# A gated two-layer transformer on one core: attention 0 reordered, attention 1's queries prepared three units ahead on ScalarE

## The chip, the core and the metric

The kernel is one program on one core of a Trainium2 chip. The core has five engines that run their own instruction streams and meet through semaphores: TensorE (PE, matrix products and transposes; PEld is its weight load), VectorE (DVE), ScalarE (ACT), GpSimd (POOL) and SyncE (SP, here a queue that issues DMAs). The metric is the device time of one execution in microseconds, lower is better. The median of three executions of the kernel before is 2252.59 us (2250.19 to 2254.02).

## The reference, cut to what matters

Four batches of 512 tokens with 512 channels pass four layers. Each is `x = x + tanh(g) * f(layernorm(x))`:

```
attention 0:  kv  = ctx @ W_k.T + b_k                     # 512 x 128 per batch
              sim = (xn @ kv) @ kv.T * scale              # 512 x 512
              f   = softmax(normalise_rows(sim) * gamma + beta)
mixture 0:    8 experts, 2 chosen per token, and a shared network of 1024
attention 1:  16 heads of 32 in 4 groups; keys and values are the 4 x 32 columns of ctx
              f   = (softmax(q @ k.T / sqrt(32)) @ v) @ Wc.T + bc
mixture 1:    16 experts, 6 chosen per token, and a shared network of 704, with biases
```

`layernorm` subtracts the mean of a token's 512 channels and divides by their deviation; it has no parameters. All is float32; where TensorE is to be fast and exact, a number is split into a high and a low part (`hi`, `lo`) and the products of the parts are summed.

## The kernel before, in words

The four layers run one after another in blocks of their own; all engines meet between blocks. `x` stays in SBUF as `x_res`, 16 tiles of 128 tokens, four for a batch. Nothing is scheduled by a planner: each engine's instructions stand in the order in which the code writes them, and an engine that waits holds back everything behind it.

**Statistics.** `row_stats` (VectorE, L104 to L118) takes a batch's sums, ScalarE's `deviation` (L125) takes the root of the variance in between, and the last two operations leave `rstd` and `nbias`; the next step on VectorE waits for ScalarE's answer.

**Attention 0** (L210 to L478). For each batch: the keys `kvT` (TensorE L415, ScalarE L348), their mean and centred copy `kc` (L351, L357), `kvT` turned into `kv` (L418, L353); the normalised rows `xn` (L130) turned into `pT` (L425, L363); the product `oT` (L429, L367), the scores (L436) into PSUM banks 0 to 3; ScalarE squares them (L373) and takes the root (L376), VectorE scales and adds (L449 to L465), ScalarE takes the exponent (L381), VectorE adds the result to `x_res` (L470 to L476). TensorE does the keys, the turning, the product and the scores of one batch after the other in a loop. ScalarE's loop body is: normalise b+1, squares b, keys b+1, turn b+1, exponents b, product b+1. Beside it GpSimd splits seven chunks of the experts' weights (`stage`, L168 to L182), and SP stores them.

**Mixture 0** begins with `row_stats` and `deviation` of batch 0 (`NORMED` = 0) and then normalises the batch's rows; batches 1 to 3 follow between the first products. The shared network comes first (L1558, L1576), then 39 blocks of 128 gathered rows. Mixture 1 has the same form with 111 blocks; its statistics of batches 0 to 2 are taken at the end of attention 1 (`NORMED` = 3).

**Attention 1** (L481 to L1050) runs 16 units, one per batch and group of four heads. A unit is eight steps j; a step scores 1024 keys by queries (TensorE L843), takes the exponent twice, as float32 and as float16 (ScalarE L792, L796), subtracts the two on GpSimd (L738) and multiplies both parts by the values (TensorE L857). Ahead of it the maxima of the scores must be known: `raw_tensor` (TensorE L828) makes raw scores that VectorE reduces (L972), half of them in the unit before (steps 0 to 3) and the first half two units before (steps 4 to 7). So the raw scores of unit u+2 begin in step 4 of unit u. They need that unit's queries as strips: GpSimd centres and scales 128 channels of `x_res` (`prepare_pool`, L686, L694, at step 5 of unit u-1), TensorE turns them (`prepare_tensor`, L817, step 0 of unit u), ScalarE and VectorE take the high and low part (L756 at step 1, L961 at step 2), and SP copies them by three DMAs of 256 KB from `qhi` and `qlo` into `qs` (`strips`, L622, L625). The maxima follow as two small DMAs (`maxima`, L632). In units 0 to 3 and 12 to 15 ScalarE and VectorE also split 16 chunks of weights (`a_stage`). The values are loaded by ScalarE's queue at the start of the block (L771) and split into three parts (L777, L723, L781, L726); the first unit's products need them.

## Time and profile before

| | |
|---|---|
| median of three executions | 2252.59 us |
| profiled execution, its own time | 2243.46 us |
| its span, first to last instruction | 2241.7 us |
| PE, PEld busy | 1911.8 (85%), 1567.9 us |
| DVE, ACT, POOL busy | 1167.9, 861.3, 1004.7 us |
| mean granted TensorE clock | 0.925 |

Busy time is what an engine executes; waiting and issuing don't count. The granted clock is a share of TensorE's full speed: 1.00 is 2.4 GHz and 0.50 is 1.2 GHz, the two levels it has; a value between is a mean over time at both. Attention 0 runs from 0 to 123 us, mixture 0 to 688, attention 1 to 1170, mixture 1 to the end.

### The profile page before, as it was taken

Reading aid. Unit: us, or ns where it says so; the run is one execution under the profiler, and the core shown is the slowest. Engines: PE = TensorE matmul, PEld = TensorE weight load, DVE = VectorE, ACT = ScalarE, POOL = GpSimd, SP = SyncE. Lnnn points to the kernel's source line nnn. Section 1 sums busy time; section 2 is a strip of 40 time slices with the busy share of each in tenths; the row PEclk is TensorE's granted clock in tenths of the full one; section 3 lists DMA queues with packets and bytes.
Section 4 is the critical chain, followed back from the end, with each engine's and each line's share of the span. In section 5 each row is a group of like instructions: output and inputs, shape, how many; then the busy total and the mean of one; then the engine's idle time right before and its main releaser. Section 6 shows DMA issues by size and latency. Waiting matters only on the chain. (4 is left out here: it accounts for less than half of the span.)

```text
span 2241.7 us, 36800 instructions
## 1 busy us (share of the span) xinstructions
PE 1911.8 (85%) x10825; PEld 1567.9 (70%) x10825; DVE 1167.9 (52%) x2331; ACT 861.3 (38%) x1403; POOL 1004.7 (45%) x735
## 2 busy tenths in 40 slices
PE   3758999979892777888868899999999979999995
PEld 2347787757671455555546777799999879899994
DVE  5474654423334896878973766444444334344442
ACT  3752221123341676767655123133333223233331
POOL 4344655625454787889631001143433323333331
PEclk9779999988895798998989999999999989999998
DMA  9367666988887574323642000766469895754444
GB/s 337 122 218 242 184 205 226 294 295 240 257 197 169 151 227 98 47 42 51 190 150 83 29 31 1 264 178 158 88 176 334 265 304 128 187 130 83 78 79 111
DMA packets 131457, 372.67 MB, mean 166 GB/s; under 512 B 20456, under 2 KB 24424, under 8 KB 126104
## 3 DMA queue, kind: packets, MB, share of 16 engines
q1 hardware_dynamic: 80504, 260.69, 36.3%
q0 software_dynamic: 33600, 79.73, 18.6%
q10 hardware_dynamic: 17184, 30.09, 3.8%
q8 instruction: 96, 1.57, 0.3%
q14 instruction: 73, 0.60, 0.1%
...
## 5 line engine op out<-in xcount | busy, mean ns | idle before, releaser
L1650 PE MATMUL ps<-f_wb,f_xThi 128*128 x2088 | 537.7, 339 | 29.9 <-issue 26.8
L1774 POOL DMA_INDIRECT y_scratch<-f_yo,f_rows x150 | 238.7, 1591 | 479.0 <-issue 264.1
L1650 PEld LDWEIGHTS ps<-f_wb,f_xThi 128*128 128x128 f32 x2088 | 372.0, 193 | 41.3 <-issue 32.3
L1650 PE MATMUL ps<-f_wb,f_xTlo 128*128 x1044 | 346.7, 332 | 0.0
L738 POOL TENSOR_TENSOR a_elo<-a_e,a_ehi 128x1024 f16<-128x1024 f32 x128 | 282.8, 2222 | 87.0 <-ACT a_ehi L796 85.0
L1669 PE MATMUL ps<-f_wb,f_hThi 128*128 (+2 forms) x822 | 276.9, 418 | 7.3 <-DVE f_hTlo L2049 7.3
L2067 DVE TENSOR_TENSOR f_g<-ps,f_bb 128x352 f32<-128x352 f32 x111 | 58.3, 525 | 337.2 <-PE ps L1650 334.4
L1747 POOL DMA_INDIRECT f_xg<-xn_scratch,f_rows x150 | 160.0, 1067 | 158.7 <-PE ps L1634 119.3
L1650 PEld LDWEIGHTS ps<-f_wb,f_xTlo 128*128 128x128 f32 x1044 | 200.9, 192 | 0.0
L1485 ACT ACTIVATE f_yo<-ps,f_share 128x512 f32<-128x512 f32 x150 | 103.2, 688 | 249.2 <-PE ps L1669 191.3
L972 DVE TENSOR_REDUCE a_nmax<-ps 128x1 f32<-128x512 f32 x256 | 163.9, 680 | 56.4 <-PE ps L828 56.0
L1558 PE MATMUL ps<-f_xhi,f_w13hi 128*128 128x512 f32 x448 | 175.7, 392 | 0.0
L1558 PE MATMUL ps<-f_xlo,f_w13hi 128*128 128x512 f32 x448 | 174.8, 390 | 0.0
L1558 PE MATMUL ps<-f_xhi,f_w13lo 128*128 128x512 f32 x448 | 174.7, 390 | 0.0
L1669 PEld LDWEIGHTS ps<-f_wb,f_hThi 128*128 128x128 f32 (+2 forms) x822 | 142.4, 191 | 42.3 <-issue 24.0
L1576 PE MATMUL ps<-f_w2hi,f_act_parts 128*128 128x512 f32 x448 | 153.0, 409 | 21.2 <-DVE x_res L2015 20.5
L828 PE MATMUL ps<-a_ks,a_qs 96*128 96x512 f32 x256 | 114.4, 515 | 61.1 <-DMA a_qs<-a_qlo 41.9
L792 ACT ACTIVATE a_e<-ps 128x1024 f32<-128x1024 f32 x128 | 132.7, 1036 | 82.5 <-PE ps L843 81.0
L1473 ACT CAST f_xThi<-ps 128x512 fp32r<-128x512 f32 x150 | 88.1, 587 | 195.1 <-PE ps L1634 187.7
L1669 PE MATMUL ps<-f_wb,f_hTlo 128*128 (+2 forms) x411 | 162.2, 395 | 0.0
L1479 ACT CAST f_hThi<-ps 128x384 fp32r<-128x384 f32 (+1 forms) x150 | 67.4, 449 | 207.5 <-PE ps L1659 202.7
L2049 DVE TENSOR_TENSOR f_hTlo<-ps,f_hThi 128x384 fp32r<-128x384 f32 (+1 forms) x150 | 78.4, 523 | 113.7 <-ACT f_hThi L1479 111.6
...
## 6 DMA issues: line engine op xcount, KB each, us to landing
...
```

Of the source, the lines that this page charges most:

```text
L738: pool.tensor_tensor(l, e, h, ALU.subtract).then_inc(lo_pool, 1)
L792: act.activation(e32[:, j % 4, :, :], ps[:, 2 * (j % 2):2 * (j % 2) + 2, :], ACT.Exp)
L828: pe.matmul(ps[:, A_BANK + n % 2, :], qs[0:3 * HD, HPG * grp + q, P * t:P * t + P], ks[0:3 * HD, grp, :], start=True, stop=True).then_inc( ...
L972: dve.tensor_reduce(nmax[:, grp % 2, n:n + 1], ps[:, A_BANK + n % 2, :], AX.X, ALU.max, negate=True).then_inc(max_done, 1)
L1473: act.copy(xThi[:, b % 2, :, :].rearrange("p k t -> p (k t)"), ps[:, XB, :]).then_inc(xT_hi, 1)
L1485: act.activation(yo[:, b % 3, :], ps[:, OB + b % 2, :], ACT.Identity, scale=share[:, b:b + 1]).then_inc(yo_ready, 1)
L1558: mm = pe.matmul(ps[:, 2 * h + w, :], wt[:, h, w, k, :], xt[:, k, S * t:S * t + S], start=(m == 0), stop=(m == 3 * KD - 1))
L1576: mm = pe.matmul(ps[:, bank(c), :], at[:, t % 2, h, P * c:P * c + P], wt[:, h, :], start=(m == 0), stop=(m == 5))
L1650: mm = pe.matmul(out, xt[:, b % 2, k, :], weights(at, w, k, low), start=(m == 0), stop=(m == 3 * KD - 1))
L1669: mm = pe.matmul(ps[:, OB + b % 2, :], ht[0:n, b % 2, P * j:P * j + P], wb[0:n, bass.ds(at + 512 * NB + 1024 * j + 512 * low, D)], start=( ...
L1747: pool.indirect_dma_start(xg[:, b % 3, :], None, xn_d, bass.IndirectOffsetOnAxis(ap=rows_of[:, b:b + 1], axis=0), bounds_check=ROWS + SPAR ...
L1774: pool.indirect_dma_start(y_d, bass.IndirectOffsetOnAxis(ap=rows_of[:, b:b + 1], axis=0), yo[:, b % 3, :], None, bounds_check=ROWS + SPARE ...
```

## The change

**Attention 0.** `kv` and `kc` get a buffer per batch, the keys use banks 4 to 7 in turn, and all four batches' keys are made ahead of the first product. The loop is written out, with no keys in it; TensorE turns batch b+1 right behind the scores of b, and the product starts as soon as the first of the four columns is copied. Batch 0 turns ahead of the third `deviation`. The statistics that mixture 0 wants of batches 0 to 2 are taken in attention 0's loop, one batch late, and `NORMED` is 3 for both mixtures.

**Attention 1.** `prepare_pool` is gone. ScalarE makes the same columns with one operation per 128 tokens (`columns_scalar`) at step 4 of the unit, four units ahead; transposes, parts and strips are made for unit u+3 at the steps where they were made for u+2. At the start three units' strips are made; the values are loaded by SP behind the strips of units 0 and 1, and ScalarE splits them behind its other first work.

```diff
-        kc = sb(ctx, "a0_kc", [P, S])
+        kc = sb(ctx, "a0_kc", [P, B, S])
...
+                act.activation(kvT[:], ps[:, 4 + 2 * (b % 2), :], ACT.Identity, bias=bk[:, 0:1],
                                accum_out=ksum[:]).then_inc(kvT_ready, 1)
                 act.wait_ge(kvT_ready, b + 1)
                 act.mul(nmean[:], ksum[:], -1.0 / S).then_inc(nmean_ready, 1)
+                act.wait_ge(nmean_ready, b + 1)
...
                 act.wait_ge(kv_tr, b + 1)
-                act.copy(kv[:].rearrange("p t d -> p (t d)"), ps[:, 5, :]).then_inc(kv_ready, 1)
-
-                act.wait_ge(nmean_ready, b + 1)
-                act.wait_ge(sim_ready, TB * b + TB)
-                act.activation(kc[:], kvT[:], ACT.Identity, bias=nmean[:, 0:1]).then_inc(kc_ready, 1)
+                act.copy(kv[:, b, :, :].rearrange("p t d -> p (t d)"), ps[:, 5 + 2 * (b % 2), :]
+                         ).then_inc(kv_ready, 1)
...
+                    act.copy(pT[:, k, :], ps[:, turned_bank(b) + k, :]).then_inc(pT_ready, 1)
...
+                    act.wait_ge(sim_ready, TB * b + t + 1)
...
+                if b > 0:
+                    g["deviation"](act, 1, b - 1)
...
                 g["deviation"](act, 0, 0)
+                normalise_scalar(act, 0)
                 act.wait_ge(par_in, PARAMS)
-                normalise_scalar(act, 0)
                 keys_scalar(act, 0)
                 g["deviation"](act, 0, 1)
+                keys_scalar(act, 1)
+                turn_scalar(act, 0)
                 g["deviation"](act, 0, 2)
-                turn_scalar(act, 0)
+                keys_scalar(act, 2)
                 g["deviation"](act, 0, 3)
+                keys_scalar(act, 3)
                 act.wait_ge(scale_in, SCALES)
                 act.activation(gates[:], graw[:], ACT.Tanh).then_inc(gates_ready, 1)
                 product_scalar(act, 0)
...
+                    if b == 0:
+                        pe.wait_ge(kv_ready, B)
+                    for k in range(KD):
+                        pe.wait_ge(pT_ready, KD * b + k + 1)
+                        mm = pe.matmul(ps[:, 4, :], kv[:, b, k, :], pT[:, k, :], start=(k == 0), stop=(k == KD - 1))
+                    mm.then_inc(oT_mm, 1)
...
+                pe.wait_ge(par_in, PARAMS)
+                keys(0)
+                keys(1)
+                turn(0)
+                keys(2)
+                keys(3)
+                for b in range(B):
+                    product(b)
+                    scores(b)
+                    if b + 1 < B:
+                        turn(b + 1)
...
-                dve.sem_inc(sim_used, TB)
...
-                with dve.Fori(0, B) as b:
+                for b in range(B):
+                    if b > 0:
+                        g["row_stats"](dve, 1, b - 1)
...
                 load(1, 1)
                 strips(0, 0)
                 strips(1, 1)
+                for b in range(B):
+                    sp.dma_start(vraw[:, TB * b:TB * b + TB, :],
+                                 a["ctx_512"][b, :, :].rearrange("(t p) d -> p t d", p=P)).then_inc(v_in, 16)
                 load(2, 2)
+                strips(2, 2)
                 sp.dma_start(wcT[:], a["a1_wcT"].rearrange("(k p) n -> p k n", p=P)).then_inc(par_in, 16)
                 sp.dma_start(bc[:], a["a1_bc"].to_broadcast([P, D])).then_inc(par_in, 16)
                 maxima(0, 0)
...
-                    if has_prepare:
-                        strips(u + 2, (grp + 2) % GROUPS)
-                        if not (static and u + 3 == UNITS):
-                            load(u + 3, (grp + 3) % GROUPS)
+                    if not (static and u + 3 >= UNITS):
+                        strips(u + 3, (grp + 3) % GROUPS)
+                        load(u + 3, (grp + 3) % GROUPS)
...
-                pool.wait_ge(g["s_ln"], 2 * B + 1)
-                for u in range(2):
-                    prepare_pool(pool, u, u, 0)
...
-                prepare_pool(pool, 2, 2, 0)
...
-                        if j == 5 and has_columns:
-                            b3 = (0 if wc_batch is None else wc_batch + 1) + (grp + 3) // GROUPS
-                            prepare_pool(pool, u + 3, (grp + 3) % GROUPS, b3)
...
+            def columns_scalar(act, u, grp, b):
+
+                wait(act, q_tr, u - 1)
+                for t in range(TB):
+                    T = TB * b + t
+                    act.activation(xc[:, grp % 2, t:t + 1, :].rearrange("p o (d q) -> p o d q", q=HPG),
+                                   x[:, bass.ds(T, 1), P * grp:P * grp + P].rearrange("p o (q d) -> p o d q", q=HPG),
+                                   ACT.Identity, scale=rstd[:, bass.ds(T, 1)],
+                                   bias=nbias[:, bass.ds(T, 1)]).then_inc(xc_ready, 1)
...
+                act.wait_ge(g["s_ln"], 2 * B + 1)
+                for u in range(2):
+                    columns_scalar(act, u, u, 0)
                 keys_scalar(act, 0, 0)
                 keys_scalar(act, 1, 1)
                 prepare_scalar(act, 0, 0)
+                columns_scalar(act, 2, 2, 0)
+                prepare_scalar(act, 1, 1)
+                columns_scalar(act, 3, 3, 0)
+                prepare_scalar(act, 2, 2)
+                g["deviation"](act, 2, 2)
                 act.wait_ge(v_in, 16 * B)
                 act.copy(v_hi, v_raw).then_inc(vhi_ready, 1)
-                prepare_scalar(act, 1, 1)
-                g["deviation"](act, 2, 2)
                 act.wait_ge(vres_ready, 1)
                 act.copy(v_mid, v_res).then_inc(vmid_ready, 1)
                 maxima_scalar(act, 0, 0)
                 g["deviation"](act, 2, 3)
+                act.wait_ge(g["s_ln"], 2 * B + B)
...
-                        if j == 1 and has_prepare:
-                            prepare_scalar(act, u + 2, (grp + 2) % GROUPS)
+                        if j == 1 and not (isinstance(u, int) and u + 3 >= UNITS):
+                            prepare_scalar(act, u + 3, (grp + 3) % GROUPS)
+                        if j == 4 and not (isinstance(u, int) and u + 4 >= UNITS):
+                            columns_scalar(act, u + 4, grp, b + 1)
...
+                pe.wait_ge(qlo_ready, 2)
+                prepare_tensor(pe, 2, 2)
                 raw_tensor(pe, 0, 0, range(16))
-                pe.wait_ge(qlo_ready, 2)
+                pe.wait_ge(qlo_ready, 3)
...
+                    turns = not (isinstance(u, int) and u + 3 >= UNITS)
...
-                        if j == 0 and has_prepare:
+                        if j == 0 and turns:
                             if last_job(grp, b):
                                 job_read(pe, *last_job(grp, b))
                             else:
                                 pe.wait_ge(mlo_ready, u + 1)
-                            prepare_tensor(pe, u + 2, (grp + 2) % GROUPS)
+                            prepare_tensor(pe, u + 3, (grp + 3) % GROUPS)
...
                             if job(grp, 2, b):
                                 job_read(pe, *job(grp, 2, b))
                             else:
-                                pe.wait_ge(qlo_ready, u + 3)
+                                pe.wait_ge(qlo_ready, u + 4)
...
+                prepare_vector(dve, 2, 2)
...
-                        if j == 2 and has_prepare:
-                            prepare_vector(dve, u + 2, (grp + 2) % GROUPS)
+                        if j == 2 and not (isinstance(u, int) and u + 3 >= UNITS):
+                            prepare_vector(dve, u + 3, (grp + 3) % GROUPS)
...
-    NORMED = B - 1 if layer == 1 else 0
+    NORMED = B - 1
```

TensorE in attention 0, before: the loop's body up to the product (ps is PSUM, a_xn the normalised rows, a_pT these turned; ISA and REGISTER_ALU rows are the loop's waits).

```order
L415 MATMUL ps<-a_ctxT,a_wkT 128x512
L416 REGISTER_ALU
L418 MATMUL ps<-ident,a_kvT 128x128 x4
L423 ISA
L425 MATMUL ps<-ident,a_xn 128x128 x4
L423 REGISTER_ALU
L425 MATMUL ps<-ident,a_xn 128x128 x4
L423 REGISTER_ALU
L425 MATMUL ps<-ident,a_xn 128x128 x4
L423 REGISTER_ALU
L425 MATMUL ps<-ident,a_xn 128x128 x4
L429 MATMUL ps<-a_pT,a_kv 128x512 x4
```

And after, from the last batch's keys on:

```order
L426 MATMUL ps<-a_ctxT,a_wkT 128x512
L431 MATMUL ps<-ident,a_kvT 128x128 x4
L450 MATMUL ps<-a_pT,a_kv 128x512 x4
L461 MATMUL ps<-a_kc,a_oT 128x512 x4
L440 MATMUL ps<-ident,a_xn 128x128 x16
L450 MATMUL ps<-a_pT,a_kv 128x512 x4
L461 MATMUL ps<-a_kc,a_oT 128x512 x4
L440 MATMUL ps<-ident,a_xn 128x128 x16
```

The keys' two rows have left the loop; scores of a batch (L461) and the turning of the next (L440) now stand side by side.

ScalarE at the start of attention 1, before (a_v is the values' parts, a_vraw their load, a_ks the keys, a_qhi the queries' high part):

```order
L771 DMA a_vraw<-in_ctx_dram 128x4x128 x4
L750 CAST a_ks<-a_kraw 96x512 x2
L756 ACTIVATE a_qhi<-ps 128x512
L777 CAST a_v<-a_vraw 128x64x32
L756 ACTIVATE a_qhi<-ps 128x512
L125 ACTIVATE std<-vraw,eps 128x4
L781 CAST a_v<-a_vres 128x64x32
L762 CAST a_mhi<-ps 16x128
L125 ACTIVATE std<-vraw,eps 128x4
L792 ACT_TABLE_LOAD
```

And after:

```order
L768 ACTIVATE a_xc<-x_res,nbias,rstd 128x128 x8
L761 CAST a_ks<-a_kraw 96x512 x2
L777 ACTIVATE a_qhi<-ps 128x512
L768 ACTIVATE a_xc<-x_res,nbias,rstd 128x128 x4
L777 ACTIVATE a_qhi<-ps 128x512
L768 ACTIVATE a_xc<-x_res,nbias,rstd 128x128 x4
L777 ACTIVATE a_qhi<-ps 128x512
L125 ACTIVATE std<-vraw,eps 128x4
L803 CAST a_v<-a_vraw 128x64x32
L805 CAST a_v<-a_vres 128x64x32
L783 CAST a_mhi<-ps 16x128
L125 ACTIVATE std<-vraw,eps 128x4
```

Sixteen column operations are new (L768), the load is gone from this queue, and both value copies (L803, L805) moved behind three units' queries. The copy of the maxima (a_mhi) stands behind them as before.

ScalarE in unit 0 around steps 3 to 6, before (a_e and a_ehi are the two exponents):

```order
L796 ACTIVATE a_ehi<-ps 128x1024
L172 CAST a_stage_down<-a_later_raw 128x512
L792 ACTIVATE a_e<-ps 128x1024
L796 ACTIVATE a_ehi<-ps 128x1024
L792 ACTIVATE a_e<-ps 128x1024
L796 ACTIVATE a_ehi<-ps 128x1024
L168 CAST a_stage_up<-a_later_raw 128x4x4x32
L762 CAST a_mhi<-ps 16x128
L792 ACTIVATE a_e<-ps 128x1024
L796 ACTIVATE a_ehi<-ps 128x1024
```

And after:

```order
L821 ACTIVATE a_ehi<-ps 128x1024
L172 CAST a_stage_down<-a_later_raw 128x512
L817 ACTIVATE a_e<-ps 128x1024
L821 ACTIVATE a_ehi<-ps 128x1024
L768 ACTIVATE a_xc<-x_res,nbias,rstd 128x128 x4
L817 ACTIVATE a_e<-ps 128x1024
L821 ACTIVATE a_ehi<-ps 128x1024
L168 CAST a_stage_up<-a_later_raw 128x4x4x32
L783 CAST a_mhi<-ps 16x128
```

Four column operations stand between the exponents of step 4 and step 5, in each unit up to 11; the rest is unchanged.

## Rows read from the trace of the kernel before

In the windows a row gives start:end and length, then the busy us of PE, PEld, DVE, ACT and POOL with their instruction counts, the granted clock, the DMA share and GB/s. In the lines a row is line, engine, operation, tiles, shapes and count, then busy us and mean ns of one, then the engine's idle time ahead of them and what ended it. In the timeline it is start, duration, engine, line, operation.

**Rows 1.** windows, two stages: busy PE, PEld, DVE, ACT, POOL; clock; DMA

```profile
122.00:688.00 566.00, 494.33 (x2280) 397.30 (x2280) 245.30 (x522) 168.64 (x320) 289.01 (x258) 0.93 0.78 237
735.00:1142.00 407.00, 329.81 (x2735) 224.63 (x2735) 338.04 (x524) 289.70 (x363) 330.23 (x168) 0.88 0.48 119
```

**Rows 2.** windows, attention 1 by units (0-3, 4, 7-8, 9-10, 11, 12-15)

```profile
735.00:840.50 105.50, 79.04 (x648) 55.97 (x648) 97.37 (x147) 79.06 (x105) 88.25 (x44) 0.85 0.70 194
840.50:868.90 28.40, 18.98 (x174) 13.76 (x173) 14.30 (x31) 16.66 (x21) 20.63 (x11) 0.82 0.58 156
...
920.70:967.10 46.40, 37.86 (x347) 27.66 (x346) 33.84 (x63) 33.81 (x41) 42.63 (x23) 0.89 0.32 43
967.10:1017.90 50.80, 45.51 (x363) 28.27 (x362) 42.48 (x67) 33.14 (x40) 40.73 (x22) 1.00 0.25 39
1017.90:1041.20 23.30, 19.24 (x175) 14.18 (x174) 17.75 (x33) 17.16 (x22) 21.42 (x12) 0.85 0.32 43
1041.20:1140.60 99.40, 81.12 (x653) 54.37 (x652) 88.47 (x120) 75.34 (x97) 74.67 (x36) 0.85 0.58 163
```

**Rows 3.** waits, attention 1: who waited for whom, total us, times, longest

```profile
PE ps L828 <- DMA a_qs<-a_qlo: 34.2, 9, 8.3
```

**Rows 4.** lines, attention 1: xcount | busy us, mean ns | idle before

```profile
L738 POOL TENSOR_TENSOR a_elo<-a_e,a_ehi 128x1024 f16<-128x1024 f32 x128 | 282.8, 2222 | 87.0 <-ACT a_ehi L796 85.0 <-POOL a_ks L701 1.3
L996 DVE TENSOR_TENSOR a_otok<-a_osum,a_rden 128x128 f32<-128x128 f32 x62 | 62.5, 1008 | 0.4
L686 POOL TENSOR_TENSOR a_xc<-x_res,rstd 128x512 f32 (+1 forms) x13 | 17.9, 1373 | 0.0
L694 POOL TENSOR_TENSOR a_xc<-a_xc,nbias 128x512 f32<-128x512 f32 x13 | 14.7, 1128 | 2.6 <-POOL a_xc L686 2.6
L762 ACT CAST a_mhi<-ps 16x128 fp32r<-16x128 f32 x15 | 3.7, 249 | 23.0 <-PE ps L833 23.0
```

**Rows 5.** timeline, attention 0: start us, us, engine line op, count, [idle before <-releaser]

```profile
36.00 5.74 PE L429 MATMUL ps<-a_pT,a_kv 128*128 128x512 f32 x8 [14.97 <-ACT a_pT L363]
41.77 0.60 ACT L367 ACTIVATE a_oT<-ps 128x512 f32<-128x512 f32 x1 [2.19 <-PE ps L429]
42.42 3.70 PE L436 MATMUL ps<-a_kc,a_oT 128*128 128x512 f32 x8 [0.69 <-ACT a_oT L367]
51.23 3.67 PE L425 MATMUL ps<-ident,a_xn 128*128 128x128 f32 x16 [0.75 <-ACT a_kv L353]
...
92.73 0.18 DVE L449 RECIPROCAL a_rstd<-a_sdev 128x4 f32<-128x4 f32 x1 [7.56 <-ACT a_sdev L376]
98.90 0.27 DVE L465 TENSOR_SCALAR a_nmx<-a_mx 128x1 f32<-128x1 f32 x2
105.98 0.60 ACT L367 ACTIVATE a_oT<-ps 128x512 f32<-128x512 f32 x1 [1.25 <-PE ps L429]
```

**Rows 6.** timeline, first 34 us, VectorE

```profile
21.66 11.82 DVE L110 TENSOR_TENSOR mdif<-mdif 128x4 f32<-128x4 f32 x1
```

**Rows 7.** timeline, start of mixture 0

```profile
123.39 1.28 ACT L125 ACT_TABLE_LOAD   x1 [2.83 <-PEq L272]
127.55 1.52 ACT L130 ACTIVATE f_xn<-x_res,nbias,rstd 128x512 f32<-128x512 f32 x2 [0.57 <-DVE nbias L118]
143.43 0.30 ACT L125 ACTIVATE std<-vraw,eps 128x4 f32<-128x4 f32 x1 [3.52 <-DVE vraw L112]
147.58 0.78 PE L1558 MATMUL ps<-f_xhi,f_w13hi 128*128 128x512 f32 x1
```

**Rows 8.** timeline, start of attention 1

```profile
708.29 3.94 POOL L723 TENSOR_TENSOR a_vres<-a_vraw,a_v 128x2048 f32<-128x2048 f32 x1 [0.84 <-PE ps L817]
715.90 1.22 PE L828 MATMUL ps<-a_ks,a_qs 96*128 96x512 f32 x2 [7.64 <-DMA a_qs<-a_qlo]
729.71 0.25 ACT L762 CAST a_mhi<-ps 16x128 fp32r<-16x128 f32 x1 [12.84 <-PE ps L833]
735.05 1.02 ACT L792 ACTIVATE a_e<-ps 128x1024 f32<-128x1024 f32 x1
```

94 lines of the change are left out of this document (38 added, 56 removed).

## The prediction

> **What bounds the kernel now.** I read the windows by stage first. In mixture 0 TensorE is busy for 494.3 of 566.0 us [rows 1]; the change touches nothing of it but its start, and nothing of mixture 1. Attention 1 takes 407 us with no engine full: VectorE 338.0, GpSimd 330.2, TensorE 329.8, ScalarE 289.7, at a granted clock of 0.88 [rows 1]. Split by units [rows 2] it has three kinds. Units 0 to 3: VectorE 97.4 of 105.5 us, so VectorE sets the pace. Units 9 and 10, and 5 and 6 like them: TensorE 45.5 of 50.8 us, at full clock. Units 4, 7, 8 and 11 (98.1 us): TensorE idles at a clock of 0.82 to 0.89, GpSimd is busy for 84.7. The waits name one cause: TensorE's raw scores wait 34.2 us, in 9 places, for the strips of the low part [rows 3]. In attention 0 the timeline shows a chain that runs from engine to engine: the first `oT` copy at 41.77, the fourth at 105.98, so 21.4 us per batch [rows 5].
>
> **Attention 0, the loop.** It loses the keys, whose handing to and fro stood between scores and product. I lay the new loop out from one `oT` copy to the next. ScalarE: copy 0.6, four normalisations at 0.76 [rows 7], four squares at 0.6, like the copy of as many columns [rows 5], a table load of 1.28 (as [rows 7] shows one) and one or two roots of 0.30: VectorE gets the deviation at 7.5 to 7.8. VectorE needs 6.4 us from there to the last maximum (92.73 to 99.17) [rows 5]: 14.1. Two exponents follow, 1.6 by the normalisations' length, then the copy: 15.8. TensorE's path is shorter: 0.65, scores 3.7, turning 3.67, the first column's copy 0.6, product 5.74 [rows 5]: 14.4. The moved `row_stats` of a batch fits between VectorE's last addition and the next deviation, but its root stands ahead of that deviation on ScalarE, 0.3 us. I take 16.0 per batch, three times: (21.4 - 16.0) x 3 = -16.2 us; at the end +0.3.
>
> **Attention 0, the start.** Before, VectorE stood for 11.82 us in an operation on 128 x 4 numbers [rows 6], and ScalarE behind it. Now ScalarE turns batch 0 ahead of that wait. But the first product needs all four batches' keys, and the last of them stands on ScalarE behind the fourth `deviation`. If the stall comes back on a later statistics operation (GpSimd's run of work is where it was), the fourth root comes at about 37.3 and the keys take 3 us more: product at 40.3, against 36.00 [rows 5], +4.3. Without the stall 36, +0. Nothing in the trace decides; I take +2.5. Sum of attention 0: -13.4, between -17 and -5.
>
> **Mixture 0's start.** ScalarE's first instruction is at 123.39, the rows begin at 127.55, 4.16 us later [rows 7]; with statistics ready they begin at +0.35: -3.8. Later ScalarE stands 3.52 us for the third batch's statistics, and the logits' copy behind it [rows 7], of which 3.0 were behind the logits' end; that wait goes too. The first expert product, at 147.58 or +24.2 [rows 7], comes at about +17.4: -6.8. What is late next is the expert weights' load, asked for at the block's start. If that binds only half is won: -7.5 to -2.
>
> **Attention 1, the start.** Values no longer compete with the keys' load, and ScalarE does the columns at once: I expect the first strips 2 us earlier than their landing before 715.90 [rows 8]. Against this, the DMA queue holds a third unit's strips (3 x 256 KB) and the values ahead of the maxima's small copies, and ScalarE's copy of the maxima, at 729.71 before [rows 8], stands behind both value copies, which end at about 731.5 (the values in at 723.5, behind six strips; a copy of some 2 us, GpSimd's subtraction of 3.94 [rows 8], a second copy). So the first exponent, 735.05 before [rows 8], comes at 736.9: +1.8, between -3 and +5.
>
> **Attention 1, the units.** GpSimd loses 1.37 + 1.13 = 2.50 us per unit [rows 4]. ScalarE gains four operations of 128 x 128. Below they cost 0.25 each, what a 16 x 128 copy takes [rows 4], above 0.76, the 128 x 512 form with the same scale and bias [rows 7]. I take 0.40: the lower row has the same length, and a scale and a bias read from memory come on top. So 1.6 us per unit, 1.0 to 3.0. ScalarE has room: 79.1 of 105.5 us at its fullest [rows 2].
>
> The strips get a whole unit more, so the 34.2 us of waits go. What is late next differs by kind.
> - Units 4, 7, 8, 11: GpSimd (84.7 - 10.0) / 4 = 18.7 us, ScalarE (67.6 + 6.4) / 4 = 18.5, TensorE at full clock about 16.4 (its busy time by its clock). Three engines near 18 don't fit perfectly; I take 20.5 per unit: 82.0 for 98.1, -16.
> - Units 0 to 3: VectorE idles 8.1 us in all [rows 2]. Part of it goes, and with less work on GpSimd a little of VectorE's waiting for it: its operation L996 has a mean of 1008 ns [rows 4] for 128 x 128 numbers. I take -7.
> - Units 5, 6, 9, 10: TensorE's own work leaves 5.3 us of 50.8 [rows 2]; with somewhat fewer waits for VectorE -2.6 over both pairs.
> - Units 12 to 15: 99.4 us, VectorE 88.5; unit 13 no longer prepares. -2.4.
>
> Together -28; the ends are -38 (20.5 becomes 19.3, and VectorE's waits halve) and -12 (new waits between the engines take the place of most).
>
> A rule that speaks against the move: the Trainium skill (ScalarE: Activation LUTs, Rules for kernel authors) gives additions and multiplications to VectorE, not ScalarE. In units 0 to 3 this trace has VectorE at 92% and ScalarE at 75% [rows 2]. By the rule the work would be on VectorE and lengthen those units; by the rows it belongs where it is put.
>
> **Sum.** -13.4 - 6.8 + 1.8 - 28 = -46.4. The profiled execution took 2243.46 us, 9.1 below the median of 2252.59; 2243.5 - 46.4 = 2197.1 there, and 2206 for the median.
>
> **Rivals.**
> A: the engines block each other where the strips' wait stood. VectorE with two operands in SBUF waits for GpSimd already (L996, mean 1008 ns, 62 times [rows 4]), and eight columns of L738 at 2222 ns are 17.8 us per unit. For it: in units 0 to 3 only 8.1 us of VectorE's time are free. Against: units 4, 7, 8, 11 have VectorE at 14 to 18 us. Units then give -10 in place of -28: 2252.6 - 28.4 = 2224.
> B: the long stall [rows 6] strikes inside attention 0's loop, where two of the moved `row_stats` now run beside GpSimd's splitting: 2 x 11.8 = +23.6, so 2252.6 - 22.8 = 2230. The stall ended when GpSimd's run of work ended, and stretched over many of its instructions. For it: in the old place it did happen. Against: it happened once, and the batches end beyond most of GpSimd's work. The Trainium skill (SBUF, State Buffer, Who interferes with whom) says that the blocked side waits while the other's instruction holds the pair. By it each such wait would be one instruction of GpSimd, at most 2.2 us here, and the total 2 x 5 x 2.2 = 22 at the very worst; the row's 11.82 us doesn't agree with a wait for one instruction.
> C, slower: the clock. TensorE's 329.8 us in attention 1 are at 0.88 [rows 1], 290 at full clock. If shorter, more evenly spread pauses kept it at 0.7, it would be busy 414 us and with some 40 of waits take 454: +47 in place of -28, 2252.6 - 18.4 + 47 = 2281. It turns slower than before as soon as the units lose more than 18 us, a clock below some 0.75 (290 / 385). For it: 0.82 in unit 4 after a wait of 8.3 us [rows 2, 3]. Against: what preceded the low clock there was idle time, which the change takes away.
> D: the change doesn't do what it says. The wait is only booked on the strips, and something behind them (the maxima of the same unit) binds at once: the units give 0, so 2252.6 - 18.4 = 2234.
> E: all ends good: -17 - 7.5 - 3 - 38 = -65, 2188.
>
> **How the numbers follow.** Forecast (sum between -36 and -56) 0.55, A 0.20, B 0.07, C 0.03, D 0.05, E 0.07; the last 0.03 is for a loss that I don't see. The time is the first's, 2206; its own range is 2196 to 2217. The range of 8 in 10 reaches E and over A, B and D: 2187 to 2236. What lies outside is C, the unseen, and the far ends of the others, 2 in 10 at most. A measurement here tells about 0.2% (4.5 us) from no change: faster is all but C, the unseen and a little of D: 0.92; same 0.03; slower 0.05.
>
> **What would show it.** In the profile after: `oT` copies 16 us apart, the first at 42 to 46; attention 0 ending near 110; no root in mixture 0's first 20 us, first expert product 17 us behind the block's start; in attention 1 no TensorE wait for `a_qlo` behind unit 0, units 4, 7, 8, 11 near 20.5 us, GpSimd at 19 us per unit, the column operations at 0.4 us; a clock above 0.9 from unit 4 on. The forecast is wrong if the strips' wait goes and another of its size stands under DVE `a_nmax` or ACT `a_ehi` (A), if a statistics operation takes over 5 us (B), or if the clock falls (C).

## The result, and the profile after

The changed kernel took 2214.5 us (median of 6 runs, 2210.7 to 2224.1); beside it the kernel before took 2251.4 (2237.6 to 2261.3). The ratio is 0.9843, with a 95% interval of 0.9816 to 0.9870: 37 us faster, 8.5 us behind the forecast of 2206 and inside its range. A second series gave the same two kernels 2227.0 against 2252.9, ratio 0.9875 (0.9846 to 0.9904). Over both, the 12 runs of the changed kernel have a median of 2219.7: some -33 us. The difference is clear of the noise; its size is known to some 5 us only.

The profiled execution after took 2224.05 us (span 2222.2, granted clock 0.923), the slowest of its six, and the one before was 9 us quicker than its median. A difference of these two executions (19.4 us) tells too little. So I read the instants that divide the stages off the timelines of all the profiles that were taken: oT copies, first expert product, first statistics of attention 1, its first and last exponent. The first two columns are the two executions that the prediction speaks of. The means are over every profile whose code for that stage, and for what starts it, is the old or the new.

| stage, us | before | after | old code, mean (profiles) | new code, mean (profiles) | difference | forecast |
|---|---|---|---|---|---|---|
| start to the first oT copy | 41.8 | 44.6 | 42.0 (3) | 45.3 (6) | +3.3 | +2.5 |
| first to fourth oT copy | 64.2 | 52.8 | 63.3 (3) | 52.2 (6) | -11.1 | -16.2 |
| fourth copy to first expert product | 41.6 | 40.4 | 41.2 (3) | 40.0 (6) | -1.3 | +0.3 - 6.8 |
| first expert product to attention 1's statistics | 540.8 | 545.8 | 543.0 (3) | 546.3 (6) | +3.3 | 0 |
| statistics to first exponent | 46.7 | 47.3 | 46.3 (3) | 47.4 (7) | +1.1 | +1.8 |
| attention 1's units | 405.6 | 378.7 | 406.2 (3) | 377.2 (6) | -29.1 | -28 |
| mixture 1 | 1101.0 | 1112.7 | 1101 to 1118 in all fourteen | | 0 | 0 |
| sum | | | | | -33.7 | -46.4 |

The sum of the means agrees with the timing. In the row from the first expert product on, old and new profiles overlap (540.8 to 544.3 against 542.1 to 552.8), so its +3.3 is not clear of the spread. Now the stages in the profile after. The timeline of attention 0 (start us, us, engine line op, count, [idle before <-releaser]):

```profile
24.08 9.19 DVE L117 TENSOR_SCALAR rstd<-inv 128x4 f32<-128x4 f32 x1
31.99 1.25 POOL L182 TENSOR_TENSOR a_stage_down<-a_stage_raw,a_stage_down 128x512 fp32r<-128x512 f32 x1
36.62 0.30 ACT L125 ACTIVATE std<-vraw,eps 128x4 f32<-128x4 f32 x1 [10.65 <-DVE vraw L112]
39.43 5.11 PE L450 MATMUL ps<-a_pT,a_kv 128*128 128x512 f32 x8 [0.68 <-ACT a_kv L364]
44.57 0.60 ACT L375 ACTIVATE a_oT<-ps 128x512 f32<-128x512 f32 x1 [3.68 <-PE ps L450]
61.05 0.57 ACT L375 ACTIVATE a_oT<-ps 128x512 f32<-128x512 f32 x1
63.29 3.39 DVE L513 SCALAR_TENSOR_TENSOR x_res<-a_y,a_coef,x_res 128x512 f32<-128x512 f32 x2
80.25 0.57 ACT L375 ACTIVATE a_oT<-ps 128x512 f32<-128x512 f32 x1
```

The stall is back on another statistics instruction, 9.19 us on 128 x 4 numbers, and ends at 33.27 with GpSimd's last subtraction of its run (33.24). Three periods follow, 16.5, 19.2 and 17.1 us (the fourth copy is at 97.39), where I had laid out 16.0. In the second, two additions to x that need 1.41 us beside an idle GpSimd take 3.39. But in the third GpSimd runs nothing at all and no operation of VectorE is stretched. VectorE waits 4.08 us for a root on ScalarE, and ScalarE before that for TensorE's scores. The scores of this batch (first row), and of the same batch in act_cols_2 (second row; a run of experiment 2, with the same attention 0):

```profile
80.93 6.52 PE L461 MATMUL ps<-a_kc,a_oT 128*128 128x512 f32 x8 [6.26 <-issue]
82.56 3.67 PE L461 MATMUL ps<-a_kc,a_oT 128*128 128x512 f32 x8 [2.35 <-issue]
```

They take 6.52 us at a granted clock of 0.56 in the one and 3.67 at 1.00 in the other. The four batches of the profile after have 3.67, 5.89, 6.52 and 6.49 us, and TensorE stood idle for 0.73, 5.60, 6.26 and 3.87 us just before them; in the kernel before it was 3.70 us each time, behind 0.69 us of idle time. The new order made this pause: the product of a batch now runs early, so that nothing stands right before its scores. The squares on ScalarE wait for the scores, and VectorE gets the deviation 9.7 to 10.1 us behind the oT copy and not the 7.45 of the first period. The third period of the six profiles with this attention 0 follows it: 17.3, 17.1 and 17.4 us with scores of 6.7, 6.5 and 6.7, then 16.0 and 15.9 with 5.4 and 5.3, and 14.9 with 3.67. The length of the pause alone doesn't settle the clock: before the last scores it was 3.64 us in stats_in_mixture, and they took 3.67, and 3.87 us in the profile after, where they took 6.49.

The start of mixture 0 in the timeline, against [rows 7]:

```profile
117.25 0.39 SPq L1281 DMA_DIRECT2D f_gw<-in_f_gateT_dram  x1
117.31 1.52 ACT L130 ACTIVATE f_xn<-x_res,nbias,rstd 128x512 f32<-128x512 f32 x2 [2.73 <-PEq L271]
125.25 1.05 ACT L1369 CAST f_w13hi<-f_wraw 128x1024 fp32r<-128x1024 f32 x1 [0.81 <-DMA f_wraw<-in_f_w_dram]
127.70 1.04 ACT L1369 CAST f_w13hi<-f_wraw 128x1024 fp32r<-128x1024 f32 x1 [1.40 <-DMA f_wraw<-in_f_w_dram]
130.50 0.63 PE L1557 MATMUL ps<-f_xhi,f_gwlo 128*128 128x512 f32 x1
132.57 0.81 ACT L130 ACTIVATE f_xn<-x_res,nbias,rstd 128x512 f32<-128x512 f32 x1 [1.64 <-DMA xn_scratch<-f_xn]
133.79 0.59 ACT L1378 COPY f_lgT<-ps 128x512 f32<-128x512 f32 x1 [0.40 <-ACT f_xn L130]
137.75 0.54 PE L1589 MATMUL ps<-f_xhi,f_w13hi 128*128 128x512 f32 x1
```

The rows begin at once, and no root is there. But the first product comes 20.5 us behind the block's start, not 17.4: the logits are done at 131.1 and their copy waits on ScalarE to 133.79. ScalarE has stood 0.81 and 1.40 us for the load of the experts' weights, f_wraw, for which it did not wait before, and then 1.64 us for the store of an earlier f_xn, where it waited for the statistics before. All six profiles with this code have these three waits (0.8 to 1.8, 1.4 to 1.5, 1.2 to 1.7 us).

Attention 1 by the same kinds of units as [rows 2] (units 0 to 3; 4; 5 and 6; 7 and 8; 9 and 10; 11; 12 to 15), in the windows view (length, busy us of each engine, clock, DMA share, GB/s):

```profile
730.80:832.40 101.60, 80.33 (x647) 57.77 (x648) 94.36 (x144) 86.58 (x120) 76.42 (x36) 0.79 0.74 203
832.40:855.60 23.20, 20.09 (x174) 15.09 (x174) 18.95 (x34) 18.68 (x25) 17.68 (x9) 0.85 0.78 202
855.60:903.20 47.60, 43.96 (x363) 28.25 (x362) 38.72 (x67) 36.80 (x47) 37.01 (x19) 1.00 0.26 43
903.20:945.40 42.20, 35.62 (x348) 25.97 (x347) 35.23 (x61) 37.37 (x50) 36.74 (x19) 0.96 0.36 49
945.40:993.10 47.70, 44.07 (x363) 28.29 (x362) 39.14 (x69) 36.85 (x48) 37.44 (x19) 1.00 0.27 42
993.10:1013.40 20.30, 17.67 (x174) 13.49 (x173) 17.46 (x33) 18.78 (x25) 18.66 (x10) 0.92 0.36 50
1013.40:1109.50 96.10, 78.41 (x653) 53.46 (x652) 83.42 (x120) 74.41 (x96) 72.89 (x34) 0.88 0.54 161
```

The waits in it, where [rows 3] had 34.2 us for the strips (who waits for whom: us, times, longest):

```profile
PE ps L855 <- DVE a_nmax L1002: 21.9, 20, 2.9
PE ps L884 <- DVE a_osum L1018: 16.9, 12, 2.9
```

And two groups of the lines view, beside [rows 4]:

```profile
L1026 DVE TENSOR_TENSOR a_otok<-a_osum,a_rden 128x128 f32<-128x128 f32 x62 | 60.3, 973 | 0.4
L768 ACT ACTIVATE a_xc<-x_res,nbias,rstd 128x128 f32 (+1 forms) x48 | 25.8, 637 | 0.0
```

The strips' waits are gone. What TensorE waits for now is VectorE: its maxima, sums and rows of a_otok together held it for 28.2 us before (14.7 + 10.2 + 3.3) and for 45.4 after (21.9 + 16.9 + 6.6), so that 17 of the 34 us came back in pieces of 2.9 us at most. GpSimd is at 296.8 / 16 = 18.6 us per unit, as forecast. A column operation takes 25.8 / 48 = 0.54 us of ScalarE (0.64 us from its start to its end; they overlap).

### The profile page after: what moved, and what is told of

Its sections match the earlier page's. It is cut to its first block and busy times, and to the rows that moved or that the text cites. A ratio compares the mean times of both kernels' runs of the same rounds, so it can differ in the third digit from the quotient of the medians.

```text
span 2222.2 us, 36653 instructions
## 1 busy us (share of the span) xinstructions
PE 1907.8 (86%) x10825; PEld 1568.1 (71%) x10825; DVE 1152.9 (52%) x2331; ACT 891.1 (40%) x1466; POOL 967.7 (44%) x703
## 5 line engine op out<-in xcount | busy, mean ns | idle before, releaser
L1681 PEld LDWEIGHTS ps<-f_wb,f_xThi 128*128 128x128 f32 x2088 | 373.7, 194 | 40.7 <-issue 31.7
L752 POOL TENSOR_TENSOR a_elo<-a_e,a_ehi 128x1024 f16<-128x1024 f32 x128 | 282.2, 2217 | 82.7 <-ACT a_ehi L821 80.4
L1516 ACT ACTIVATE f_yo<-ps,f_share 128x512 f32<-128x512 f32 x150 | 103.3, 689 | 253.9 <-PE ps L1700 189.8
L1607 PE MATMUL ps<-f_w2hi,f_act_parts 128*128 128x512 f32 x448 | 154.0, 411 | 23.3 <-DVE x_res L2046 22.4
L884 PEld LDWEIGHTS ps<-a_v,a_ehi 128*128 128x128 f16 x1024 | 96.1, 105 | 63.1 <-DVE a_osum L1018 33.4
L855 PE MATMUL ps<-a_ks,a_qs 96*128 96x512 f32 x256 | 109.7, 498 | 34.5 <-DVE a_nmax L1002 27.9
## 6 DMA issues: line engine op xcount, KB each, us to landing
f_wb<-w_scratch SPq DMA_DIRECT2D x8, 1536.0 KB, 10.2
```

The source lines that it names most:

```text
L752: pool.tensor_tensor(l, e, h, ALU.subtract).then_inc(lo_pool, 1)
L855: pe.matmul(ps[:, A_BANK + n % 2, :], qs[0:3 * HD, HPG * grp + q, P * t:P * t + P], ks[0:3 * HD, grp, :], start=True, stop=True).then_inc( ...
L884: mm = pe.matmul(ps[:, PV_BANK, P * t:P * t + VC], part[:, j % 4, i, P * t:P * t + P], v3[:, bass.ds(TB * b + 2 * (j % 2) + i, 1), grp, 0:VC],
L1516: act.activation(yo[:, b % 3, :], ps[:, OB + b % 2, :], ACT.Identity, scale=share[:, b:b + 1]).then_inc(yo_ready, 1)
L1607: mm = pe.matmul(ps[:, bank(c), :], at[:, t % 2, h, P * c:P * c + P], wt[:, h, :], start=(m == 0), stop=(m == 5))
L1681: mm = pe.matmul(out, xt[:, b % 2, k, :], weights(at, w, k, low), start=(m == 0), stop=(m == 3 * KD - 1))
```

## The experiments

**1. The halves by themselves.** att0_only puts the old `cross_attention_1` into the changed kernel, att1_only the new one into the kernel before.

```
-def cross_attention_1(...):   # the changed one
+def cross_attention_1(...):   # the one of before          (att0_only; att1_only the other way)
```

> The changed kernel with attention 1 as it was before the change: only attention 0 and mixture 0's statistics are new. Theory S (the stages add up): the profiles after and before differ by -9.9 us from the start to mixture 0's first expert product (first oT copy +2.8, three batches -11.4, the end +2.4, mixture 0's start -3.7), and this all reaches the end, so about 2241 against 2251, ratio 0.9956, between 0.994 and 0.997. Rival R (given back later): mixture 0's experts took 545.8 us after and 540.8 before, from first product to first statistics; if they end by the transfers of the weights and not by TensorE, half or all of the gain is lost there: ratio 0.998 to 1.000, and then attention 1 alone must give some -32 to -37 us. In the profile S wants the stretch from the first expert product to attention 1's first statistics at 541 us, as before, R at 546 or more.

> The kernel before with attention 1 of the changed kernel; attention 0 and mixture 0's statistics are as before. Theory S: attention 1's units gave -26.9 us between the two profiles and its start +0.6, so -26.3: about 2225 against 2251, ratio 0.988, between 0.986 and 0.990. Rival R: -32 to -37, ratio 0.984 to 0.986. In the profile the units take 379 us (first exponent to last statistics) and mixture 1 the 1101 us that it took before; if mixture 1 takes 1112 us again, the changed attention 1 has lengthened it.

Measured: att0_only 2247.6 (12 runs) against 2255.2, ratio 0.9978 (0.9956 to 1.0000); att1_only 2220.7, ratio 0.9855 (0.9828 to 0.9882). By the ratios attention 1 is worth some -33 us and attention 0 some -5 (by the medians -34.5 and -7.6). att1_only's ratio lies in R's range and below S's, att0_only's between the two; the intervals reach into both theories' ranges. The profile of att0_only has its first expert product at 139.3, 8.3 us earlier than before, and its first exponent at 731.0, 4 us earlier: mixture 0 took 545.9. So part of the gain is lost there, as R has it, not all. In att1_only the units took 374.3 us, 5 less than S expected. Mixture 1 took 1114 us in both, not S's 1101; the profiles of experiment 4 bear on this.

**2. The lead and the move apart.** pool_cols_3 keeps the lead of three units and gives the columns of units 4 to 15 back to GpSimd; act_cols_2 keeps the columns on ScalarE and goes back to two units.

```
 pool_cols_3, GpSimd:  + if j == 5 and u + 4 < UNITS: columns_pool(pool, u + 4, grp, b + 1)
              ScalarE: - if j == 4 ...: columns_scalar(act, u + 4, grp, b + 1)
 act_cols_2, SP:       - strips(u + 3, ...)            + strips(u + 2, ...)
             ScalarE:  - prepare_scalar(act, u + 3, .) + prepare_scalar(act, u + 2, .)   (TensorE, VectorE alike)
```

> The changed kernel, but with the columns of units 4 to 15 on GpSimd again (two wide operations behind its sixth subtraction of a unit), still three units ahead; the first four units' columns stay on ScalarE. Theory L (the lead of a unit is what gains): the strips' waits stay away, and GpSimd is busy for 2.5 us more of each of 12 units, 21 to 21.5 us per unit. Units 0 to 3 and 12 to 15, where VectorE sets the pace, and 5, 6, 9, 10, where TensorE does, change by under 2 us together; units 4, 7, 8, 11 become GpSimd's at 21.2 to 22.5 us, 87 to 90 for 85.7. So +3 to +6 us over the changed kernel, about 2219, ratio 0.986 to the kernel before. Rival M (the move off GpSimd is what gains): of the 27 us of the units 15 or more come from GpSimd's 2.5 us times 16 less, the units then take 394 us and more, 2230, ratio 0.991.

> The changed kernel, but turned and copied into strips two units ahead as before (columns made one unit less ahead too), with the columns on ScalarE. Theory L: TensorE's waits for a_qlo are back at 25 to 35 us in some 9 places, units 4, 7, 8, 11 take 94 to 98 us in all, the units 395 to 402 us: 2233 to 2238, ratio 0.992 to 0.994 to the kernel before. Rival M: the strips' wait returns only in part because GpSimd no longer delays the low parts, units at 384 to 388 us, about 2222, ratio 0.987. The values are loaded behind two units' strips, so attention 1's first exponent comes up to 2 us earlier than in the changed kernel by either.

Measured: pool_cols_3 2239.4, ratio 0.9929 (0.9897 to 0.9961); act_cols_2 2239.1, ratio 0.9937 (0.9916 to 0.9958). Of the units' -27 us between these two profiles (405.6 to 378.7) each edit alone gives a part: 398.9 and 395.1 us. By kinds of units:

| units, us | GpSimd, two (before) | GpSimd, three | ScalarE, two | ScalarE, three (after) |
|---|---|---|---|---|
| 0 to 3 | 105.4 | 111.5 | 105.1 | 101.6 |
| 4, 7, 8, 11 | 98.1 | 85.0 | 96.0 | 85.6 |
| 5, 6, 9, 10 | 102.6 | 103.3 | 96.2 | 95.4 |
| 12 to 15 | 99.5 | 99.1 | 97.8 | 96.1 |

The second row is the lead's, -13 against -2 for the move alone. For act_cols_2 theory L came out in its waits, its units and its ratio; its waits show TensorE again at

```profile
PE ps L853 <- DMA a_qs<-a_qlo: 33.9, 9, 5.6
```

The third row is the move's alone, -6 to -8, and there my theory L was wrong for pool_cols_3 (and so were its 87 to 90 for the second row: GpSimd had the room). The units' 398.9 us and the time are worse than even M's 394 and 2230. Units 5 and 6 of pool_cols_3 in the windows and lines views:

```profile
865.10:916.40 51.30, 45.57 (x364) 28.30 (x364) 42.84 (x67) 33.20 (x40) 43.27 (x24) 1.00 0.24 40
...
L1044 DVE TENSOR_TENSOR a_otok<-a_osum,a_rden 128x128 f32<-128x128 f32 x8 | 9.5, 1188 | 0.0
```

and the same two units of the profile after:

```profile
L1026 DVE TENSOR_TENSOR a_otok<-a_osum,a_rden 128x128 f32<-128x128 f32 x8 | 5.5, 686 | 0.0
```

The eight multiplications that read two tiles in SBUF lose 4 us, as much as the pair of units (51.3 to 47.6) and as VectorE's busy time (42.8 to 38.7). GpSimd no longer runs the four column operations of the pair (2.7 + 2.1 us), and the multiplications are caught beside one of its instructions less often: alone they take 0.28 us, caught up to 1.9.

The first row needs both edits: the lead alone costs 6 us, together they win 4. The lines view of these units names where, in pool_cols_3 and in the profile after (VectorE's part of the weights' splitting):

```profile
L182 DVE TENSOR_TENSOR a_stage_down<-a_later_raw,a_stage_down 128x512 fp32r<-128x512 f32 x7 | 18.3, 2615 | 0.0
L182 DVE TENSOR_TENSOR a_stage_down<-a_later_raw,a_stage_down 128x512 fp32r<-128x512 f32 x7 | 4.7, 678 | 0.0
```

In pool_cols_3 each of the seven starts some 0.1 to 0.3 us behind a GpSimd subtraction (L770) and takes 2.6 us; after, each takes 0.68. Before the change half of the eight took 1.82, beside GpSimd's column operations. That is 13.6 us more of VectorE, whose waits TensorE then has: 27.5 us there, 18.8 after. The cost is one of timing between two engines; no run moves only this operation.

**3. The stall at the start.** late_staging makes GpSimd wait for the fourth row_stats before it splits anything; att0_early leaves the stall and puts the first product, its scores and squares ahead of keys 2 and 3 (in banks 6 and 7). all_starts has both, and two edits in attention 1. after_again is the changed kernel again, the control of this series.

```
 late_staging, GpSimd:  + pool.wait_ge(g["s_ln"], B)
 att0_early, TensorE:     turn(0); - keys(2); keys(3); product(0); scores(0)
                                   + product(0) (waits kv_ready 1); scores(0); keys(2); keys(3)
             ScalarE:     turn_scalar(0); + normalise(1); product_scalar(0); squares(0); deviation(2); keys(2); ...
 all_starts, att. 1:      VectorE row_stats(2, 2) ahead of prepare_vector(2); ScalarE maxima_scalar(0) ahead of v_mid
```

> The changed kernel once more, as the control of this call and for a second profile of it. Both theories: ratio to the kernel before 0.984, between 0.982 and 0.987, some 2215. What it tells apart is what of the first profile belongs to the kernel and what to one execution: the units at 379 +- 3 us; mixture 1 again at 1110 to 1115 us, as in five profiles of five different kernels, so that the 1101 of the kernel before was the exception (theory S: mixture 1 is not touched), or at 1101 (rival: its length goes its own way from execution to execution).

> The changed kernel, with GpSimd's splitting of the bias rows and of the weights in attention 0 held back until all four row_stats are done. Theory P (the stall is GpSimd's run of wide operations: it ended at 33.19 with GpSimd's last subtraction at 33.24, and at the same place before): no operation on 128 x 4 takes over 0.7 us, batch 3's root comes at 27.6 and not at 36.6, the first product at some 30.5, the first oT copy at 35.6 and not at 44.6, -9; GpSimd catches up, since it idles for 44 us at the end of attention 0, but more of its work stands beside VectorE's in the first batch, +1 to +3: in all -6 to -8 us, ratio 0.981. Rival Q (the stall is something else of the start, a load that lands late on a shared queue, or the first use of an instruction): the stall stays at 9 us under another statistics operation and the first oT copy at 44 to 46, ratio 0.984 to 0.986.

> The changed kernel with attention 0's beginning in another order: the first product, its scores and their squares come ahead of the third and fourth batch's keys and deviations, which go to banks 6 and 7. The stall stays. Theory E (what the stall holds back is only the chain through batch 3's root): the first product starts at 24 to 25 and the first oT copy is at 29 to 31 and not at 44.6; VectorE begins batch 0's y at 37.5 to 38.5 and not at 52, and the second oT copy comes at 50 to 54 and not at 61: -8 to -10 us at the second copy and everywhere behind it, ratio 0.980. Rival F (it comes back behind the copy): keys 2 and 3 and the tanh now stand on ScalarE between deviation and exponents, and TensorE turns batch 1 only behind them: second copy at 57 or later, under -4 us, ratio 0.982 to 0.984.

> Both edits of attention 0's beginning (GpSimd's splitting held back, first product ahead of the last keys), and in attention 1 batch 2's statistics moved ahead of the third unit's low parts (VectorE idles there for 6.0 us) and the maxima's copy ahead of the second value copy on ScalarE. Theory: without the stall the statistics end near 28, y of batch 0 starts at 34 to 35, the second oT copy at 48 to 51: -10 to -12 us; attention 1's first exponent comes 42.5 to 43.5 us behind the first statistics and not 47.3, -4; in all -14 to -16 us, ratio 0.977 to 0.978, about 2200. Rival: mixture 0's experts hand half of it back (from first product to statistics 545 us and more with the earlier start, 541 to 544 with the later ones so far): -8, ratio 0.981.

Measured against 2252.9: after_again 2227.0, ratio 0.9875 (0.9846 to 0.9904); late_staging 2217.3, 0.9833 (0.9804 to 0.9862); att0_early 2212.6, 0.9820 (0.9788 to 0.9853); all_starts 2217.3, 0.9828 (0.9796 to 0.9860). The control missed its range by a hair; its units (381.0 us) and its mixture 1 (1111.9) are as expected. P is shown: the timeline of late_staging has

```profile
25.84 0.17 DVE L117 TENSOR_SCALAR rstd<-inv 128x4 f32<-128x4 f32 x1
30.88 1.26 POOL L333 TENSOR_TENSOR a_b2s<-a_b,a_b2s 16x512 fp32r<-16x512 f32 x1
35.57 0.60 ACT L376 ACTIVATE a_oT<-ps 128x512 f32<-128x512 f32 x1 [2.27 <-PE ps L451]
50.51 0.57 ACT L376 ACTIVATE a_oT<-ps 128x512 f32<-128x512 f32 x1
53.42 2.73 DVE L514 SCALAR_TENSOR_TENSOR x_res<-a_y,a_coef,x_res 128x512 f32<-128x512 f32 x2
59.61 1.25 POOL L182 TENSOR_TENSOR a_stage_down<-a_stage_raw,a_stage_down 128x512 fp32r<-128x512 f32 x1
71.44 0.57 ACT L376 ACTIVATE a_oT<-ps 128x512 f32<-128x512 f32 x1
```

No stall, and the first copy at the 35.6 that I expected (batch 3's root at 29.4 for 27.6, the product at 31.8 for 30.5). The first period is 14.9 us, with scores of 3.67 and GpSimd idle for most of VectorE's part of it (42.8 to 47.8); the second, beside GpSimd's deferred work and with scores of 6.5, 20.9, of which VectorE is busy for 20.2 (windows). Of the 9.0 and 9.4 us won at the first copy 8.3 and 9.2 are left at the first expert product (129.4 against 137.8 and 138.7). In att0_early the first copy is at 28.3 and the second at 48.6, and the product comes at 125.8; By these instants E is right, F wrong; the ratio lies between the two. all_starts has them at 26.3 and 45.8, but 68.5 and 87.9 behind that: without the stall GpSimd's work meets VectorE in the loop, where two additions to x took 5.96 us, and its product (129.0) is 3 us later than with att0_early alone. Its theory (0.977) is missed and its rival met, 0.981 with mixture 0 at 545 us and more; in attention 1 the first exponent came 46.8 us behind the statistics and not the 42.5 to 43.5 expected, on which the next experiment bears. The intervals of the three overlap that of the control; for their order the instants in the profiles speak, not the timing. Mixture 0 took 548.0 to 551.1 us in these three, and 541 to 546 in most of the others (552.8 in after_again).

**4. The mixtures, the moved statistics, and attention 1's start.** before_again is the kernel before; stats_in_mixture has row_stats of batches 0 to 2 back in mixture 0; start_queue and early_and_queue change attention 1's start.

```
 stats_in_mixture:  - NORMED = B - 1                      + NORMED = B - 1 if layer == 1 else 0
                    - row_stats(dve, 1, b - 1), deviation(act, 1, b - 1)   (attention 0)
 start_queue, SP:   - wcT, bc; maxima(0, 0)               + maxima(0, 0); wcT, bc   (waited for from unit 4 on)
              and the two edits of all_starts in attention 1; early_and_queue adds att0_early
```

> The kernel before once more, for a second profile of it. Theory S: its ratio is 1.000 within 0.3%, and mixture 1 takes 1110 to 1118 us, as in the nine profiles of other kernels, none of which changes mixture 1; the 1101 of the first profile were that one execution. Mixture 0 takes 541 to 544 us from first expert product to attention 1's statistics, with 15 to 18 us of waits for gathered rows, as in the two profiles with the old attention 0. Rival R2: mixture 1 takes 1101 again, then the old start together with the old attention 1 really leaves it shorter by 11, and mixture 0 545 or more would say that the longer waits for gathered rows don't come from attention 0's earlier end.

> The changed kernel with batch 0 to 2's row_stats back at mixture 0's start. Theory W (the wait that they left is taken by another, so the move gains little): mixture 0's first expert product comes 24 us behind the block's first instruction, as before, against 20.5 with them moved; attention 0's loop is 0 to 1 us shorter per batch without them, 51 to 52.8 for three, and its end 1 to 2 us shorter. From the fourth oT copy to the first product 41.5 to 43 us against 40.3 and 40.7. In all 0 to +2 us to the changed kernel. Rival V (the move is worth the 6.8 us that were forecast): from the fourth copy to the product 46 or more.

> The changed kernel, with three edits at attention 1's start: batch 2's statistics ahead of the third unit's low parts, the maxima's copy on ScalarE ahead of the second value copy, and the loads of wcT and bc (1.25 MB) issued behind the maxima's two small copies and waited for only from unit 4 on. Theory K (the maxima's copies stood behind these transfers: in the run before with the first two edits the low parts of the maxima were ready at 718.2 and on their way at 718.9, and TensorE waited 5.67 us for them, to 724.3): the wait falls to about 2.1 us, as where the queue is empty, and the first exponent comes 42.5 to 43.5 us behind the first statistics, not 46.8 to 47.3. -4 us to the changed kernel. Rival N (it is the values and the third unit's strips, 1.8 MB, that fill the queue): TensorE waits 4 us or more and the first exponent stays at 45 to 47.

> The first product ahead of the last keys in attention 0, and the three edits at attention 1's start: the version that the runs point to. From att0_early (2213, ratio 0.982) and theory K's -4: about 2208, ratio 0.980, 0.977 to 0.983. Rival: mixture 0's waits for gathered rows and the rest of the program give it back, ratio 0.983 and more.

Measured against 2252.5: before_again 2253.4, ratio 1.0009 (0.9989 to 1.0028); stats_in_mixture 2224.4, 0.9877 (0.9837 to 0.9916; 4 runs); start_queue 2219.5, 0.9858 (0.9829 to 0.9888); early_and_queue 2209.4, 0.9824 (0.9792 to 0.9856).

before_again took 1110.9 us in mixture 1 and 544.3 in mixture 0: the 1101 was not the kernel's. But start_queue and early_and_queue had 1104.5 and 1101.7 with the same mixture 1, so its length goes its own way over 17 us, for a cause that no run shows. TensorE's wait for gathered rows in mixture 0 stood at 17.5, 15.6 and 22.9 us (first, att1_only, this profile) with the old attention 0, and in this run it is

```profile
PE ps L1634 <- DMA f_xg<-xn_scratch,f_rows: 22.9, 9, 5.1
```

With the new one it was 19.6 to 27.3. The groups overlap. That mixture 0 hands back some 3 us when it starts 9 us earlier, and 6 when it starts 19 us earlier (548.9, the mean of the four), is what the means say. The gathers may be a part of it, but att0_early had the shortest wait of the new ones, 19.6, with a mixture 0 of 548.0; the cause is open.

stats_in_mixture decides the moved statistics. Its first product comes 39.6 us behind the fourth oT copy, where the changed kernel has 40.4 and 40.7 and W expected 41.5 to 43, and its loop took 50.6. Without the moved statistics attention 0's end, from the fourth copy to mixture 0's first instruction, is 16.6 us and mixture 0's start 23.0; with them 18.7 to 20.0 and 20.5 to 20.8. Most of the end's difference is TensorE's clock: the last scores took 3.67 us here and 5.4 to 6.6 in the others. So W is right that the move gains little: from the first copy to the product it takes 90.2 us, where the six profiles with the statistics moved took 90.6 to 93.7, and the timing (0.9877, the control's 0.9875) sees no difference. V is refuted.

start_queue gives K half. The timeline of its start of attention 1:

```profile
720.50 0.28 DVE L1008 TENSOR_TENSOR a_mlo<-ps,a_mhi 16x128 fp32r<-16x128 f32 x1 [0.84 <-ACT a_mhi L783]
723.37 1.22 PE L870 MATMUL ps<-a_qs,a_ks 98*128 98x512 f32 x2 [2.14 <-DMA a_qs<-a_mlo]
723.66 3.94 POOL L743 TENSOR_TENSOR a_v<-a_vres,a_v 128x2048 bf16<-128x2048 f32 x1 [2.01 <-ACT a_v L806]
723.73 3.88 DVE L112 SCALAR_TENSOR_TENSOR vraw<-mdif,vraw 128x4 f32<-128x4 f32 x1
729.26 1.02 ACT L817 ACTIVATE a_e<-ps 128x1024 f32<-128x1024 f32 x1
```

The maxima's copies land in 2.14 us (5.67 in all_starts, where wcT and bc were ahead of them), so N's reason is wrong, though its 45 to 47 us came true. A statistics instruction of 128 x 4 meets GpSimd's 3.94 us subtraction of the values, ends with it, and the root on ScalarE stands ahead of the first exponent: 46.6 us behind the statistics instead of 47.3. The gain became a stall. In the changed kernel the same subtraction met batch 3's statistics at another operation (L106) and held it for 0.41 us.

early_and_queue has the lowest median of the study, 43 us below before, and met its range. Its ratio does not differ from att0_early's 0.9820; it lies 0.002 below the 0.9843 of the changed kernel in its first series and 0.005 below the control's; the intervals overlap, so that it beats the changed kernel is likely by its instants (first product at 127.1, first exponent at 721.9 against 730.8 and 738.8), not shown by the times. The three edits at attention 1's start add nothing that can be seen: att0_early has its first exponent at 721.1 without them.

## Why the prediction was right, point by point

- **The units, -28.** Right in sum, -29.1, and from the waits that were named, though that the sum is so near is luck, since errors of 4 us in the kinds cancel: the strips' 34.2 us are gone with half of them back as short waits for VectorE. By kinds (means of three old and six new profiles): units 4, 7, 8, 11 -14.4 for -16; units 0 to 3 -5.0 for -7; units 12 to 15 -2.7 for -2.4; units 5, 6, 9, 10 -6.9 for -2.6. The last is the mis-sized one: I looked at TensorE's 45.5 of 50.8 us and took the rest as all there was, but its work itself was stretched by its waits for VectorE, and VectorE was waiting for GpSimd. Taking four pairs of column operations off GpSimd was worth 7 us in these four units, though GpSimd had time to spare there (40.7 of 50.8 us in a pair).
- **Columns 0.40 us each.** Measured 0.54, 2.2 us per unit for 1.6, inside the 1.0 to 3.0. ScalarE had the room.
- **The rule of the Trainium skill against the move.** ScalarE: Activation LUTs, Rules for kernel authors, gives such arithmetic to VectorE. No run put it there; the move from GpSimd to ScalarE gained 7 us in units 5, 6, 9 and 10, so ScalarE was the better place of the two that were run; VectorE as the third stays untested.
- **Attention 0's loop, -16.2.** Measured -11.1: 17.4 us per batch, not 16.0. The layout itself was sound: where neither of two things got in its way, act_cols_2's third period, it took 14.9 us with a moved row_stats in it. Two terms were mis-sized. I let VectorE's 6.4 us stand as in [rows 5], where GpSimd was idle; beside GpSimd's splitting VectorE took 7.7 us in the first period and 8.1 in the second, and there its additions to x were stretched as well, so that the moved row_stats ended only when the deviation was due. It is rival B's mechanism in small pieces, without its 11.8 us. And I let TensorE's scores stand at 3.7 us, the row's at full clock, and called its path the shorter; at a granted clock near 0.6 they took 5.3 to 6.7 us and held back ScalarE's root. The third period's 17.1 us against 14.9 are that. It is what rival C names, in another stage than the one where I looked for it.
- **Attention 0's start, +2.5.** Measured +3.3, by the case that was written down: the stall on a later statistics instruction, root at 36.6 for 37.3, product at 39.4 for 40.3.
- **Mixture 0's start, -6.8, and attention 0's end, +0.3.** Measured -1.3 together, as large a miss as the loop's. By means of the same profiles, mixture 0's first product came 20.6 us behind the block's start for 23.8 before, -3.2, inside the -7.5 to -2 and near the half that I gave if the weights' load binds. It does bind, 2.2 us in the profile after; a store that a normalisation waits for, 1.6 us, I did not name. Attention 0's end grew by 1.9 us and not 0.3, mostly by the slow scores of the last batch. stats_in_mixture shows that moving the statistics was worth nothing in all.
- **Not in the sum:** mixture 0 took 3.3 us longer, not clear of its spread.
- **Attention 1's start, +1.8.** Measured +1.1. Unit 0's strips were there 23.3 us behind the first statistics, for 27.5 before, but VectorE spent this on batch 2's row_stats, while TensorE waited 4.86 us for it. That the values' copies would hold the maxima's was wrong: the second one ended at 724.4, and ScalarE then stood 0.67 us for the maxima.
- **The clock** was above 0.9 in units 5 to 11, but 0.85 in unit 4 and 0.88 in the last four, and 0.79 in units 0 to 3, where it had been 0.85. In attention 1 rival C did not happen.

So -46.4 became -33: of the 13 us, 5 are the loop, 5 attention 0's end and the start of mixture 0, 3 mixture 0 itself. The 2214.5 of the first series lies in the forecast's own range of 2196 to 2217, the 2219.7 of all twelve runs does not. Rival A's 2224 lies nearer to that than the forecast's 2206, but not for its reason: its short waits for VectorE are there, yet the units gave all that was forecast.
